# One core, four layers: raw rows sent to the experts and normalised there, the second layer reordered, one barrier, one step and two table waits fewer

## The chip, the cores and the metric

The kernel runs on one core of a Trainium2 chip. A core has five engines that work side by side, each through its own instructions in the order in which they were written: TensorE (matrix products and transposes, into PSUM), VectorE, ScalarE (activations), GpSimd (here small arithmetic and the scatter transfers) and SyncE (it starts transfers). They wait for each other on semaphores. The metric is the device time of one execution in microseconds, the median of several runs. Before the change it is 975.71 us, from 974.56 to 979.03 in three runs.

## The reference

Input `x` is 16 rows of 256 positions of 128 numbers, 4096 tokens. Four layers follow, each a residual around a layer norm (mean and variance over the 128 numbers, no gain):

```python
x = x + attn_a(_layernorm(x))   # q, k, v = x@W + b; 16 heads of 8; softmax within blocks of 64 positions
x = x + ffn(_layernorm(x))      # logits = x@Wr (8 experts); the top 2, softmax of the two;
                                # out = sum of weight * (silu(x@Wg) * (x@Wu)) @ Wd / sqrt(12), hidden 512
x = x + attn_b(_layernorm(x))   # xt = x@w_tor.T + b; q, k, v from xt; attention over the 16 rows of the
                                # input, with a bias of 1 on the diagonal and its two neighbours (cyclic);
                                # then @ out_w.T + out_b
x = x + ffn(_layernorm(x))      # the same expert weights again
```

Everything is fp32. Only the two chosen experts of a token are computed by the kernel.

## The kernel before, in words

Six stages follow each other: `setup`, `first_layer` (first attention, and the routing of its result), `experts`, `second_layer`, `experts` again, and `combine`. `finish` stands between them: GpSimd clears the stage's semaphores, and a barrier over all engines follows (L1790) on top of the one with which a stage's block ends.

**Setup** loads weights and the input (into `stream`, 32 tiles of 128 tokens), folds the torus matrix into Q, K and V, and writes eight empty tiles into the table `routed`.

**First layer.** It works in 16 pairs of tiles; four tiles are a quad, `c = p // 2`. For each `p` every engine has its list, with the work of other quads between: TensorE scores pair p+1, mixes and flips pair p-1 and turns pair p; VectorE takes the maximum (`peak`) and subtracts it (`shift`) for two half groups, divides pair p-2, and in between measures and routes older quads; ScalarE does the exponentials and nearly all copies out of PSUM. Routing of a quad: the sum is measured (`measure2`), GpSimd takes the root (`root2`), VectorE writes a normalised row into `norm_x` (`normalise2`, L672), TensorE transposes it (`turn_x2`) and makes the logits, VectorE finds the top two (`route`), TensorE counts ranks (`route_ranks`), VectorE finds each token's place (`spots`), and GpSimd sends each row twice into `routed` with an indirect DMA (`dispatch`, L441). A row has 132 numbers: the 128, the token, the first expert, and two weights. Beside this the expert weights are loaded and split into a high part (ScalarE, `weight_high`) and a low part (GpSimd, `weight_low`, L434), two a quad from pair 2 to pair 17. At its end a table of which expert and which rows each expert step takes is made.

**Experts.** 72 steps of 128 rows; the steps of an expert follow each other. In a step SyncE loads 128 rows (four buffers; a buffer is free when the step four back is weighed), TensorE transposes them (`turn`), ScalarE and VectorE split them into high and low, TensorE makes gate and up with three products each, ScalarE the Silu (L1669), VectorE the product; TensorE transposes it (`cross`) and multiplies it down; VectorE weighs it and GpSimd scatters the result (L1581). TensorE works one to three steps apart from the others. After four written-out steps it is a loop of four steps a pass.

**Second layer.** It works in eight quads; one round of the lists belongs to a quad `c`, and it is called a step here. The sum of residual and expert results is made (`join`) and goes into `stream`; GpSimd adds the output bias to it (`bias_out`, L1018). TensorE's list in a step: scores(c+1) first half, ranks(c-5), mixing(c-1) first half, two turns, K(c+2), flip(c-1), `turn_back`(c-2), logits(c-4), scores(c+1) second half, mixing second half, Q(c+2), two turns, `map_out`(c-2), V(c+1), flip, `turn_x2`(c-3), `turn_x`(c+3). VectorE's: maximum and shift of the first half (L1302, L1309), divide(c-2) second half, measure, weights and spots of c-5, maximum and shift of the second half, divide(c-1) first half (L1319, L1323), measure2(c-3), route(c-4), join, `add_map`(c-2) (L1331). ScalarE's: Exp first half (L1477), copy of the mixed values, two copies of the turned ones (L1485), K's copies, `out_back`, Exp second half, copy, Q's copy, two copies, the normalisation of c+3 (L1427), V's copies (L1458), the copies of the transposes `out_x2T`(c-3) and `out_xT`(c+3). GpSimd's: `root1`, `bias_out`, two tiles' dispatch of quad c-6, `root2` and a normalisation of quad c-3 (L1011), and two more tiles' dispatch (L1025).

**Combine** loads the two expert results of each token, adds both to `stream` in place, and stores.

## Time and profile before

The profiled execution took 975.18 us, its span (first to last instruction) is 973.4 us, and TensorE's granted clock was 0.88 of full speed in the mean. By the starts of the stages' first transfers:

| stage | from, us | length | TensorE | VectorE | ScalarE | GpSimd | clock |
|---|---|---|---|---|---|---|---|
| setup | 0 | 18.25 | 3.5 | 4.7 | 0.0 | 0.2 | 1.00 |
| first layer | 18.25 | 229.85 | 147.2 | 154.7 | 142.2 | 131.1 | 0.88 |
| experts | 248.10 | 221.80 | 207.0 | 119.4 | 107.3 | 69.0 | 0.97 |
| second layer | 469.90 | 256.50 | 143.8 | 114.4 | 116.8 | 127.0 | 0.75 |
| experts | 726.40 | 221.65 | 206.9 | 119.6 | 107.2 | 69.0 | 0.97 |
| combine | 948.05 | 25.35 | 0.0 | 10.7 | 0.0 | 0.0 | 0.50 |

The engines' columns are busy microseconds. An engine that is busy for nearly the whole stage bounds it; where none is, the order of the waits decides, and the timeline has to be read. A mean over a stage can hide two parts with different bounds, as the second layer does.

### The profile page before, as it was taken

How to read it: one execution, taken by the hardware profiler on the slowest of the kernel's cores; microseconds unless marked ns; L12 is line 12 of the kernel's file. 1: busy time of each engine (PE TensorE's matmuls, PEld its weight loads, DVE VectorE, ACT ScalarE, POOL GpSimd, SP SyncE). 2: the span in 40 equal slices, each digit the busy share in tenths (PEclk: the TensorE clock that was granted, in tenths of full speed). 3: DMA queues.
4: the chain of work that ended last, by engine and by line, in shares of the span. 5: the costliest groups of instructions: out<-in, count | busy, mean ns of one | idle time of the engine just before them, and what ended most of it. 6: DMA issues, size and time to landing. Idle time of an engine off the chain costs nothing. (4 is left out here: it accounts for less than half of the span.)

```text
span 973.4 us, 26881 instructions
## 1 busy us (share of the span) xinstructions
PE 708.4 (73%) x8764; PEld 583.4 (60%) x8765; DVE 523.4 (54%) x1810; ACT 473.5 (49%) x876; POOL 396.2 (41%) x458
## 2 busy tenths in 40 slices
PE   1688877831699999998077898761109999999940
PEld 1356555521588888887035676661108888888830
DVE  3367888863356555554253565642305555555524
ACT  0689877630355555553058897520005555555510
POOL 1223777786033333333231154588732333333320
PEclk9989999975799999999558999985559999999985
DMA  7001222212111111111330000001211111111107
GB/s 204 8 12 45 68 83 87 76 56 67 32 47 47 49 46 47 47 47 36 99 118 24 26 3 10 31 29 39 69 39 41 49 44 49 47 47 49 45 20 259
DMA packets 54045, 54.51 MB, mean 56 GB/s; under 512 B 8272, under 2 KB 43472, under 8 KB 53968
## 3 DMA queue, kind: packets, MB, share of 16 engines
q1 hardware_dynamic: 42608, 32.19, 12.1%
q0 software_dynamic: 8704, 18.11, 5.8%
q10 hardware_dynamic: 2656, 3.15, 0.9%
q8 instruction: 53, 0.87, 0.4%
q14 instruction: 24, 0.20, 0.1%
HBM read 29.51 MB, written 23.90 MB: 55 GB/s over the span
## 5 line engine op out<-in xcount | busy, mean ns | idle before, releaser
L1581 POOL DMA_INDIRECT expert_out<-moe_a_out,moe_a_place x72 | 69.0, 958 | 153.0 <-DVE moe_a_out L1716 153.0
L1581 POOL DMA_INDIRECT expert_out<-moe_b_out,moe_b_place x72 | 69.0, 958 | 152.7 <-DVE moe_b_out L1716 152.7
L1613 PE MATMUL wide<-wgu,moe_a_hi 128*128 x288 | 96.7, 417 | 0.5 <-issue 0.5
L1613 PE MATMUL wide<-wgu,moe_b_hi 128*128 x288 | 96.7, 417 | 0.4 <-issue 0.4
L1629 PE MATMUL wide<-wd,moe_a_hidT 128*128 x576 | 76.4, 276 | 1.1 <-DVE moe_a_out L1716 0.7
L1629 PE MATMUL wide<-wd,moe_b_hidT 128*128 x576 | 76.4, 276 | 1.0 <-DVE moe_b_out L1716 0.7
L1669 ACT ACTIVATE moe_a_glow<-wide 128x512 f32<-128x512 f32 x72 | 43.0, 598 | 69.9 <-PE wide L1613 69.8
L1669 ACT ACTIVATE moe_b_glow<-wide 128x512 f32<-128x512 f32 x72 | 43.0, 598 | 69.6 <-PE wide L1613 69.5
L441 POOL DMA_INDIRECT routed<-la_norm_x,la_place x64 | 63.6, 994 | 23.0 <-issue 19.3
L1629 PEld LDWEIGHTS wide<-wd,moe_a_hidT 128*128 128x128 f32 x576 | 70.0, 192 | 1.7 <-issue 1.7
L1629 PEld LDWEIGHTS wide<-wd,moe_b_hidT 128*128 128x128 f32 x576 | 70.0, 192 | 1.6 <-issue 1.6
L1025 POOL DMA_INDIRECT routed<-lb_norm_x,lb_place x64 | 62.2, 972 | 18.8 <-issue 18.8
L1728 DVE TENSOR_TENSOR moe_a_hid<-wide,moe_a_glow 128x512 f32<-128x512 f32 x72 | 49.8, 691 | 20.4 <-PE wide L1613 17.7
L1728 DVE TENSOR_TENSOR moe_b_hid<-wide,moe_b_glow 128x512 f32<-128x512 f32 x72 | 49.8, 691 | 20.2 <-PE wide L1613 19.1
L1613 PE MATMUL wide<-wgu,moe_a_lo 128*128 x144 | 57.4, 399 | 0.0
L1613 PE MATMUL wide<-wgu,moe_b_lo 128*128 x144 | 57.4, 399 | 0.0
L1613 PEld LDWEIGHTS wide<-wgu,moe_a_hi 128*128 128x128 f32 x288 | 49.5, 192 | 7.5 <-issue 1.0
L1613 PEld LDWEIGHTS wide<-wgu,moe_b_hi 128*128 128x128 f32 x288 | 49.4, 192 | 7.3 <-issue 0.9
L1676 ACT ACTIVATE moe_b_hidT<-wide 128x512 f32<-128x512 f32 x72 | 43.0, 597 | 13.3 <-PE wide L1621 13.3
L1676 ACT ACTIVATE moe_a_hidT<-wide 128x512 f32<-128x512 f32 x72 | 43.0, 597 | 13.1 <-PE wide L1621 13.1
L678 DVE TENSOR_REDUCE la_most<-wide 128x16 f32<-128x1024 f32 x32 | 38.7, 1209 | 19.3 <-PE wide L548 19.2
L1597 PE MATMUL wide<-const,moe_b_rows 128*128 128x128 f32 x72 | 20.0, 277 | 39.7 <-DMA moe_b_rows<-routed 39.7
(257 smaller groups left out, 1693.4 us busy)
## 6 DMA issues: line engine op xcount, KB each, us to landing
moe_a_rows<-routed SPq DMA_DIRECT2D x72, 66.0 KB, 1.9
moe_b_rows<-routed SPq DMA_DIRECT2D x72, 66.0 KB, 1.9
lb_outs<-expert_out SPq DMA_DIRECT2D x8, 512.0 KB
la_stage<-in_wg SPq DMA_DIRECT2D x8, 256.0 KB, 2.6
la_stage<-in_wu SPq DMA_DIRECT2D x8, 256.0 KB, 2.8
wd<-in_wd SPq DMA_DIRECT2D x8, 256.0 KB, 3.7
kept<-stream SPq DMA_DIRECT2D x8, 256.0 KB, 3.6
stream<-kept SPq DMA_DIRECT2D x8, 256.0 KB
```

What stands on the lines that cost most here:

```text
L441: pool.indirect_dma_start(d.routed[:, :], bass.IndirectOffsetOnAxis(ap=place[:, t, j:j + 1], axis=0), norm_x[:, t, :], None).then_inc(sent ...
L678: nc.vector.tensor_reduce(most[gp][:, :], psS[gp][:, :].rearrange("p (h k) -> p h k", k=BLK), X, ALU.max)\
L1025: pool.indirect_dma_start(d.routed[:, :], bass.IndirectOffsetOnAxis(ap=place[:, t, j:j + 1], axis=0), norm_x[:, t, :], None).then_inc(sent ...
L1581: pool.indirect_dma_start(d.expert[:, :], bass.IndirectOffsetOnAxis(ap=place[s % 4][:, 0:1], axis=0), out[u][:, :], None).then_inc(stored[ ...
L1597: nc.tensor.transpose(psX[u][:, 0:P], rows[s % 4][:, 0:D], k.ident).then_inc(turned.sem, 1)
L1613: last = nc.tensor.matmul(ps[u][:, :], x[u][:, :], w(j, part), start=i == 0, stop=i == 2)
L1629: last = nc.tensor.matmul(psY[:, 0:D], hidT[u][:, c * P:(c + 1) * P], k.wd[:, bass.ds(e, 1), c, :].rearrange("p a c -> p (a c)"), start=c ...
L1669: nc.scalar.activation(glow[s % 2][:, :], psG[s % 2][:, :], ACT.Silu).then_inc(glowing.sem, 1)
L1676: nc.scalar.activation(hidT[u][:, :], psH[:, :], ACT.Copy).then_inc(crossed_copied.sem, 1)
L1728: nc.vector.tensor_tensor(hid[u][:, :], psU[u][:, :], glow[u][:, :], ALU.mult).then_inc(hidden.sem, 1)
```

## The change

What it does, part by part:

- *Raw rows.* `norm_x` goes. `stream` gets rows of 134 numbers; the raw sum is what is transposed, sent and kept, and the four numbers of routing and two new ones, the root and minus mean times root, stand behind it. `root2` on GpSimd makes both (four operations for two). The logits of the raw row are multiplied by the root on their way out of PSUM (`take`), and `setup` takes the column means off the router's weights, so that the mean drops out. The expert stages normalise a row tile in place on ScalarE, before the transpose.
- *Second layer.* Ranks, dispatch and so on come one step earlier, dispatching two; every list has a new order. The output bias is added by TensorE: a product of ones with a tile that holds the bias in three bf16 pieces, ahead of the map's products in the same bank. `mix` has two buffers. `join` reads the residual from a tile of its own.
- *First layer.* The spot product and the rest of `spots` are two pieces, the rest behind the second shift; the weights' parts move to the first eight pairs.
- *Seams.* `finish` has no barrier of its own; the next stage takes other semaphores. 71 steps, which is the most that 8192 rows and 8 experts can need. One activation at each stage's head loads ScalarE's table.

The core of the diff:

```diff
-STEPS = 72
+STEPS = 71
-ROW = D + 4
+ROW = D + 6
 def finish(k):
     k.nc.clear_and_free_semaphores(k.used)
+    k.clearing = {s.num for s in k.used}
     k.used = []
-    k.nc.all_engine_barrier()
@@ both layers
+                nc.gpsimd.tensor_scalar(root_in2[u][:, 0, :], mom2[u][:, :, 1], EPS, None, ALU.add)
+                nc.gpsimd.tensor_scalar(root_in2[u][:, 1, :], mom2[u][:, :, 0], -1.0, None, ALU.mult).then_inc(part_rooted2, 1)
+                nc.gpsimd.tensor_tensor(rows[:, :, D + 4], root_in2[u][:, 0, :], ..., ALU.pow).then_inc(part_rooted2, 1)
+                nc.gpsimd.tensor_tensor(rows[:, :, D + 5], root_in2[u][:, 1, :], rows[:, :, D + 4], ALU.mult).then_inc(rooted2, 1)
             def turn_x2(c):
-                pe.wait_ge(normed2, c + 1)
+                pe.wait_ge(summed, 2 * c + 2)          # second layer: c + 1
+            def take(c):
+                dve.wait_ge(logits, c + 1)
+                dve.wait_ge(rooted2, c + 1)
+                nc.vector.tensor_tensor(logit[:, :, :], psX[...], scale.to_broadcast([P, BATCH, EXPERTS]), ALU.mult)
@@ first layer, VectorE, pair p
                 if even and 0 <= c - 3 < QUADS:
-                    weigh(c - 3)
-                    spots(c - 3)
-                if even and 0 <= c - 2 < QUADS:
-                    normalise2(c - 2)
+                    spot_ranks(c - 3)
                 if here:
                     peak(p, 1)
                     shift(p, 1)
+                if even and 0 <= c - 3 < QUADS:
+                    weigh(c - 3)
+                    find_places(c - 3)
@@ first layer, GpSimd (ScalarE's weight_high alike)
-                if 0 <= p - 2 < 2 * EXPERTS:
-                    weight_low(p - 2)
+                if 0 <= p + 1 < EXPERTS:
+                    weight_low(2 * p + 2)
+                    weight_low(2 * p + 3)
@@ second layer, GpSimd
+            for c in range(-3, QUADS + 5):
+                root2(c - 3)
+                dispatch((c - 5) * BATCH + 2), dispatch((c - 5) * BATCH + 3)
+                root1(c + 3)
+                dispatch((c - 4) * BATCH), dispatch((c - 4) * BATCH + 1)
@@ second layer, TensorE (new list)
+  route_ranks(c-4); route_logits(c-3); mixing(c-1,0); score(c+1,0); turn(c,0,0); turn(c,0,1)
+  project_k(c+2); flip(c-1,0); turn_back(c-2); mixing(c-1,1); score(c+1,1); map_out(c-2)
+  turn(c,1,0)  # waits for summed, c - 1, where it waited for back_copied
+  turn(c,1,1); project_q(c+2); flip(c-1,1); project_v(c+1); turn_x(c+3); turn_x2(c-2)
@@ second layer, VectorE (new list)
+  peak(c,0); shift(c,0); spot_ranks(c-4); take(c-3); weigh(c-4); find_places(c-4); measure1(c+3)
+  divide(c-1,0); peak(c,1); shift(c,1); add_map(c-2); route(c-3); count(c-3); measure2(c-2)
+  join(c+4); divide(c-1,1)
@@ second layer, ScalarE: rise_gap(c-4) first, out_xT(c+3) and then out_x2T(c-2) last, the rest as it was
             def map_out(c):
+                nc.tensor.matmul(psP[0]..., k.ones[:, :], k.offset[:, :]...to_broadcast([P, BATCH, D]), start=True, stop=False)
@@ experts, ScalarE
+            nc.scalar.activation(k.warm[:, 4:8], k.warm[:, 0:4], ACT.Silu)
+            def normalise(n, s):
+                row = rows[s % 4]
+                act.wait_ge(loaded[s % 4], (n - s % 4) * 4 + 16)
+                nc.scalar.activation(row[:, 0:D], row[:, 0:D], ACT.Identity, bias=row[:, D + 5:D + 6], scale=row[:, D + 4:D + 5])
+            normalise(0, 0), normalise(1, 1), halve(0, 0), halve(1, 1), normalise(2, 2)
             def step(n, s):
                 ... Silu(s), halve(s + 2), copy of the crossed tile (s - 1) ...
+                if s + 3 < STEPS:
+                    normalise(n + 3, s + 3)
```

(The new lists are written in short here; in the kernel each call has its bounds.)

## Rows read from the trace of the kernel before

**Rows 1.** Busy time by stretch: engine, busy us (instructions); then clock, DMA, GB/s.
```profile
300.00:350.00 50.00, 50.00 (x336) 44.51 (x335) 29.64 (x106) 25.90 (x53) 17.07 (x18) 1.00 0.18 47
570.50:586.40 15.90, 14.78 (x482) 12.29 (x471) 11.04 (x44) 14.21 (x25) 7.65 (x12) 1.00 0.02 4
643.30:717.80 74.50, 15.07 (x148) 13.72 (x140) 21.32 (x139) 3.47 (x9) 59.69 (x66) 0.55 0.16 51
```

**Rows 2.** Timeline (start, us, engine, line), GpSimd, end of the second layer.
```profile
649.74 3.12 POOL L1011 TENSOR_SCALAR lb_norm_x<-stream,lb_mom,lb_rstd 128x128 f32<-128x128 f32 x4
...
716.82 0.96 POOL L1025 DMA_INDIRECT routed<-lb_norm_x,lb_place  x1 [0.30 <-issue]
```

**Rows 3.** The page, parts 5 (costliest groups) and 6 (DMA issues).
```profile
L1669 ACT ACTIVATE moe_a_glow<-wide 128x512 f32<-128x512 f32 x72 | 43.0, 598 | 69.9 <-PE wide L1613 69.8
...
moe_a_rows<-routed SPq DMA_DIRECT2D x72, 66.0 KB, 1.9
```

**Rows 4.** Timeline, GpSimd, one step of the second expert stage.
```profile
928.91 0.96 POOL L1581 DMA_INDIRECT expert_out<-moe_b_out,moe_b_place  x1 [1.87 <-DVE moe_b_out L1716]
```

**Rows 5.** Waits (who for whom: us in total, times, longest), SyncE.
```profile
SPq L1790 <- PEq L1790: 3.0, 6, 0.8
```

**Rows 6.** Timeline, ScalarE, table loads in the two attention layers.
```profile
24.88 1.28 ACT L793 ACT_TABLE_LOAD   x1 [24.88 <-POOL la_nmr L409]
...
512.18 1.28 ACT L1477 ACT_TABLE_LOAD   x1
513.48 1.06 ACT L1477 ACTIVATE lb_prob<-lb_prob 128x1024 f32<-128x1024 f32 x1
```

**Rows 7.** Waits, TensorE, first layer, 83 to 190 us.
```profile
PE wide L484 <- DVE la_spot L737: 4.4, 4, 1.4
```

**Rows 8.** Timeline, GpSimd, end of the first layer.
```profile
217.37 1.25 POOL L434 TENSOR_TENSOR wgu<-la_stage,wgu 128x512 fp32r<-128x512 f32 x1
```

**Rows 9.** Timeline, three engines, attention steps of the second layer.
```profile
529.67 1.05 ACT L1477 ACTIVATE lb_prob<-lb_prob 128x1024 f32<-128x1024 f32 x1
...
568.04 1.07 ACT L1485 ACTIVATE lb_probT<-wide 128x512 f32<-128x512 f32 x2
569.00 1.64 ACT L1427 ACTIVATE lb_norm<-stream,lb_nmr,lb_rstd 128x128 f32<-128x128 f32 x4
570.55 1.22 DVE L1302 TENSOR_REDUCE lb_most<-wide 128x32 f32<-128x1024 f32 x1
571.17 2.55 ACT L1458 ACTIVATE lb_stand<-wide 32x512 f32<-32x512 f32 x4 [0.53 <-PE wide L1081]
574.85 1.31 PE L1183 MATMUL wide<-lb_probT,lb_stand 128*36 128x32 f32 x64
576.09 1.09 PE L1167 MATMUL wide<-const,lb_prob 128*128 128x128 f32 x8
577.02 1.02 PE L1068 MATMUL wide<-lb_xT,wqk_b 128*128 128x512 f32 x2
577.88 0.60 PE L1192 MATMUL wide<-const,lb_side 128*128 128x128 f32 x4
578.52 0.36 DVE L1319 RECIPROCAL lb_inv<-wide 128x32 f32<-128x32 f32 x1 [1.22 <-PE wide L1192]
578.76 0.96 PE L1099 MATMUL wide<-wr,lb_x2T 128*128 128x8 f32 x8
579.03 0.42 DVE L1323 TENSOR_TENSOR lb_mix<-wide,lb_inv 128x256 f32<-128x256 f32 x1
579.87 1.13 PE L1137 MATMUL wide<-lb_kz,lb_qT 32*32 32x128 f32 x64
584.65 1.13 PE L1208 MATMUL wide<-wout,lb_mixT 128*128 128x128 f32 x8 [0.48 <-ACT lb_probT L1485]
585.82 0.69 DVE L1331 TENSOR_TENSOR stream<-wide,stream 128x512 f32<-128x512 f32 x1 [3.18 <-PE wide L1208]
...
626.20 1.05 ACT L1477 ACTIVATE lb_prob<-lb_prob 128x1024 f32<-128x1024 f32 x1
```

More of the change, by code:

```diff
@@ L141, in allocate @@
     k.used = []
+    k.clearing = set()
     def sem(name):
-        k.used.append(nc.alloc_semaphore(name))
+        num = next(n for n in nc.free_semaphores if n not in k.clearing)
+        k.used.append(nc.alloc_semaphore(name, num=num))
         return k.used[-1]
@@ L192, in setup @@
         first = [(raw[:, :, :], d.w_split.rearrange("w c f -> c w f")), (cols[:, :], d.cols), (k.const[:, :], d.const[:, :]),
-                 (k.wout[:, :], d.wout)]
-        first += [(k.rows[:, r, :], d.rows[r:r + 1, :].to_broadcast([P, D])) for r in range(2)]
-        fixed = [(k.stream[:, :, :], d.x.rearrange("(t p) c -> p t c", p=P)), (k.wv[0][:, :], d.wv), (k.wr[:, :], d.wr)]
-        psF, psB = k.bank[0], k.bank[1]
+                 (k.wout[:, :], d.wout), (wr[:, :], d.wr)]
+        first += [(rows, d.rows[r:r + 1, :].to_broadcast([P, D])) for r, rows in enumerate((k.rows[:, :], row[:, :]))]
+        fixed = [(k.stream[:, :, 0:D], d.x.rearrange("(t p) c -> p t c", p=P)), (k.wv[0][:, :], d.wv)]
+        psF, psB, psE = k.bank[0], k.bank[1], k.bank[2]
         @block.sync
@@ L224, in _ @@
             nc.vector.memset(k.ones[:, :], 1.0)
-            for rows in (k.tails, spare):
-                nc.vector.memset(rows[:, :, 0:D], 0.0)
-                nc.vector.memset(rows[:, :, D + 1], -1.0)
-                last = nc.vector.memset(rows[:, :, D + 2:ROW], 0.0)
+            nc.vector.memset(k.warm[:, :], 0.0)
+            nc.vector.memset(even[:, :], 1.0 / D).then_inc(evened, 1)
+            for empty in (k.tails, spare):
+                nc.vector.memset(empty[:, :, 0:D], 0.0)
+                nc.vector.memset(empty[:, :, D + 1], -1.0)
+                last = nc.vector.memset(empty[:, :, D + 2:ROW], 0.0)
             last.then_inc(staged, 1)
+            nc.vector.memset(k.offset[:, :], 0.0)
             dve.wait_ge(weighed, 16 * len(first))
@@ L777, in _ @@
                 if not even and 0 <= c - 2 < QUADS:
+                    take(c - 2)
                     route(c - 2)
@@ L786, in _ @@
         def _(act):
+            nc.scalar.activation(k.warm[:, 4:8], k.warm[:, 0:4], ACT.Exp)
             def normalise1(c):
@@ L1420, in _ @@
         def _(act):
+            nc.scalar.activation(k.warm[:, 4:8], k.warm[:, 0:4], ACT.Exp)
             def normalise1(c):
@@ L1498, in _ @@
             act.wait_ge(cleared, 2)
-            for c in range(-3, QUADS + 6):
+            for c in range(-3, QUADS + 5):
                 here, behind = 0 <= c < QUADS, 0 <= c - 1 < QUADS
+                if 0 <= c - 4 < QUADS:
+                    rise_gap(c - 4)
                 if here:
@@ L1594, in turn @@
                 u = s % 2
-                pe.wait_ge(loaded[s % 4], (n - s % 4) * 4 + 16)
+                normed.wait(pe, n)
                 low.before(pe, n, 2)
@@ L1652, in _ @@
         def _(act):
-            for x in (high, glowing, crossed_copied):
+            nc.scalar.activation(k.warm[:, 4:8], k.warm[:, 0:4], ACT.Silu)
+            for x in (high, glowing, crossed_copied, normed):
                 x.start(act)
+            def normalise(n, s):
+                row = rows[s % 4]
+                act.wait_ge(loaded[s % 4], (n - s % 4) * 4 + 16)
+                nc.scalar.activation(row[:, 0:D], row[:, 0:D], ACT.Identity, bias=row[:, D + 5:D + 6], scale=row[:, D + 4:D + 5])\
+                    .then_inc(normed.sem, 1)
             def halve(n, s):
@@ L1753, in give @@
             eng.wait_ge(joined, n + 1)
-            eng.dma_start(crossed(d.out, n, BATCH), k.stream[:, n * BATCH:(n + 1) * BATCH, :].rearrange("p t c -> p (t c)"))\
+            eng.dma_start(crossed(d.out, n, BATCH), sums[:, n, :, :].rearrange("p t c -> p (t c)"))\
                 .then_inc(stored, 16)
```

351 lines of the change are left out of this document (182 added, 169 removed).

## The prediction

> **What bounds the kernel now.** I read the busy time by stretch first, because the stages have different limits. The expert stages are bound by TensorE: busy for 50.00 us in 50.00, with ScalarE at 25.90 [rows 1]. In the second layer a quad of attention takes 15.90 us, with TensorE at 14.78 and ScalarE at 14.21 busy, so the order on either can decide; after the last quad come 74.5 us in which GpSimd is busy for 59.69 and every other engine is nearly idle [rows 1]. The timeline of that stretch shows GpSimd's work: per quad a normalisation of 3.12 us and eight scatter transfers at 0.96 + 0.30 = 1.26 us each, the last issued at 716.82 and done at 717.8 [rows 2]. So the second layer ends by GpSimd's queue, not by attention. The chain of waits ends in the combine stage, bound by its DMAs, which the change leaves alone. My sums are made on the profiled execution: its span is 973.4 us and its time 975.18, 0.5 us under the median of 975.71.
>
> **Expert stages, both.** *One step fewer:* GpSimd's transfer row gives the period of a step, 0.96 busy + 1.87 idle = 2.83 us [rows 4]. TensorE is full, so each stage loses 2.83: -5.7. *Normalising in the stage:* one 128x128 activation a step; four of them took 1.64, so 0.41 each [rows 9]. ScalarE waits 69.9/72 = 0.97 us a step before the Silu, and the new instruction stands just ahead of that wait. It needs its rows two steps earlier than the transpose does: a row load lands 1.9 us after its issue [rows 3], and it is issued when the weighing four steps back is done, some 3 us before ScalarE comes to it. I cost it at nothing, with that wait and TensorE as its cover. Uncovered it would be 0.41 x 142 = 58 us. At a stage's start nothing covers it, the first transpose waits for the load and then for it: +0.45, twice +0.9 (0 to +1.5, if another load is waited for too). Rows longer by 8 bytes: nothing. Sum -4.8.
>
> **Barriers.** SyncE waited 3.0 us in all for the six barriers that go [rows 5], and the drains before them add a little: -3.2, between -1.5 and -4. GpSimd still clears semaphores, now beside the others; what is late next is its memset, in the second layer under 8 us of loading. The setup's added small VectorE operations lie beside its transfers: nothing, -0.5 to +1.
>
> **Tables ahead.** The first layer's load of 1.28 us stands behind the wait for the first statistics [rows 6]: it goes, -1.3. The second layer's, at 512.18, stands before the first Exp [rows 6]; the walk below deals with it. The Silu load lies beside the first gate matmuls: nothing. 512.18 + 1.28 = 513.46, and the Exp starts at 513.48 [rows 6], so a load costs its 1.28 and no more. The Trainium skill (ScalarE: Activation LUTs, "What ACT_TABLE_LOAD costs") adds a drain of about 1.38 us to every switch to another set, 2.66 in all; by it the two loads would be worth 5.3 us and not 2.6. The trace shows no such drain here, so I go by the trace.
>
> **First layer.** TensorE waited four times, 4.4 us together, for the spot product to free the bank before it could project K [rows 7]. The new order puts that product ahead of the gates' weights, and the normalisation leaves VectorE, so K comes 1.1 us earlier in pairs 8, 10, 12 and 14, which is what ScalarE waits for there: -4.5. Against it, the weights' high parts move to the first eight pairs, where ScalarE is the fuller engine; two copies are 1.07 [rows 9], and pairs 1, 3 and 5 had none: +3.2, less some waiting that takes them up, +2.5. Net -2, between -9 and +4. At the end GpSimd issues 24 transfers with hardly a gap; two low parts of 1.25 that lay among them [rows 8] leave, and the longer second root costs some 0.6: -1.9. With the table -5.2 (-12 to +2).
>
> **Second layer, GpSimd.** The normalisation (3.12 a quad) and the bias go; the root grows from two operations to four, from 1.3 to an estimated 2.0. Per quad 8 x 1.26 + 2.0 = 12.1, where it was 10.1 + 3.1 + 1.4 = 14.6. More important, dispatching starts in step 4 and not in step 6. When attention is done only 36 transfers (half of quad 3, and quads 4 to 7) and three roots are left: 45.4 + 6.1 = 51.5 us. Had attention kept its pace, the second moments of quad 5 would be there 11 us after the Exp at 626.2 [rows 9], at about 637, and the last transfer would be done at 688.5 instead of 717.8: -29.
>
> **Second layer, attention.** I think that it doesn't keep its pace. The new order puts on one chain what ran side by side: the division waits for the flip and now stands before the second maximum; the next scores wait for that shift; the output map stands behind those scores; the second pair of turns waits for the map's sum; Q is projected behind the turns; and ScalarE holds two copies, the next normalisation and V's copies behind Q's. One full step, from the copy of the second transpose to the next one, in the durations of [rows 9]: logits 0.96, mixing 1.31, scores 1.13 + 0.2 for the mask, two turns 1.09, K 1.02, flip 0.60, division 0.36 + 0.42, maximum 1.22, shift the same, scores 1.33, map 1.13 + 0.2 for the bias product, sum 0.69, turns 1.09, Q 1.02 and its copy 0.6, two copies 1.07, normalisation 1.64, V's copies 2.55, the two transposes' copies 0.55 each. That is 22 us, for steps 3 and 4. The bias product (512 columns in bf16) has no row; K is 1.02 for 512 columns in fp32, so it lies between 0.05 and 0.5, and I take 0.2, as for the mask. The other steps leave out what they lack: step 1 has no map, no second transpose and no logits, and its mixing and scores lie before its start (16.8); step 2 adds the map (19.4); step 5 loses the normalisation and its copy (20.0); step 6 has neither K nor Q (17.2). In step 0, Q behind the turns eats what the table gives, so step 1 starts at 529.7 as before [rows 9]. Then 529.7 + 16.8 + 19.4 + 22 + 22 + 20 + 17.2 = 647.1 for step 7, where the old order is at 626.2: 21 us late. The moments of quad 5 follow 11.3 us on, at 658.4, and 51.5 later the last transfer is done: 709.9, which is -7.9. I allow 1 us for stalls that the walk doesn't see: -7, between -29 (pace kept) and +10 (every full step 3 us worse). As a check, the old order walked in this manner gives 15.75 for the step that took 15.90.
>
> **Sum.** -4.8 - 3.2 - 5.2 - 7 = -20.2; 975.2 - 20.2 = 955.0 us.
>
> **The rivals.**
> *Attention keeps its pace.* Steps stay at 16 to 18 us, because the waits that I put in series are met early. For it: TensorE and ScalarE hold about 15 us of work a step [rows 1], so 16 is possible. Against: the orders are fixed in the code, and each link of the chain is a wait there. The layer then gives 29 and not 7: 933.
> *TensorE's clock (the slower side).* A step of 22 us holds 15.5 us of TensorE, 70% of it and not 93%. Where TensorE had 15.07 us in 74.5, it was granted 0.55 of full speed [rows 1], so mostly the lower level of 1.2 GHz. At that level the 11 us of TensorE on the chain would take up to 22: +10 a step. It decides from two such steps (20.2/10); five give 1005. Against: 70% lies nearer to the step that had its full clock than to that stretch.
> *The normalisation is not hidden in the experts.* If the rows came so late that it held up the Silu in every step, +58 us: 1013. Against: 0.97 of wait for 0.41 of work.
> *No change.* The second layer costs 8 us more than I walked and the first loses 4 where it gives 5: about 973.
>
> **Chances.** My forecast 0.70 (its own range 945 to 965); pace kept 0.15; clock 0.06; not hidden 0.03; no change 0.06. The range reaches down to the pace-kept case and up by the bounds of the walk: 934 to 968. 0.5%, 4.9 us, is about what a measurement can tell here. Faster is the first two and half of the last, 0.88; same 0.03; slower 0.09.
>
> **What would show it.** Right: expert steps still of 2.83 us, with ScalarE's wait before the Silu down to about 0.5; no table load ahead of the second layer's first Exp; in its steps 3 and 4 Exps about 22 us apart, with ScalarE idle for some 4 us before the copy of Q; scatter transfers from step 4 on, without a gap once attention is over. Wrong: steps of 16 to 18 us, or a granted clock near one half in them; a Silu that waits for the normalisation; expert steps of more than 2.9 us.

## The result

Median of 20 runs each: 971.47 us (966.28 to 976.82) after, 976.5 us before; the ratio is 0.9953, 95% interval [0.9933, 0.9972]. So the change makes the kernel 0.5% faster, where 955 us, 2.1% faster, was forecast. The profiled execution took 975.08 us over a span of 973.0, 3.6 us above the median of its kernel; the one of before (975.18 us, span 973.4) lies 1.3 us under its own. So the two profiles differ by 0.4 us where the medians differ by 5.0.

The spans cut at ScalarE's first Exp and at GpSimd's first and last transfer of each stage, in us:

| stretch | before | after | difference | forecast |
|---|---|---|---|---|
| start to the first layer's first Exp | 43.3 | 41.8 | -1.5 | |
| last transfer of the first layer to first one of the experts | 23.0 | 24.1 | +1.2 | |
| last one of the experts to the second layer's first Exp (before: with its table load) | 52.9 | 51.0 | -1.9 | |
| last transfer of the second layer to first one of the experts | 22.6 | 23.3 | +0.7 | |
| last transfer of the experts to the end | 34.9 | 33.4 | -1.4 | |
| these seams together | | | -2.9 | -4.9 |
| both expert stages, first to last transfer | 398.2 | 392.0 | -6.1 | -5.7 |
| first layer, first Exp to last transfer | 195.2 | 188.2 | -7.1 | -3.9 |
| second layer, first Exp to last transfer | 203.3 | 219.1 | +15.8 | -5.7 |

(Differences are taken before rounding.) The forecast column holds the prediction's terms, cut at the same places (tables, barriers and the experts' longer starts in the seams); it sums to -20.2, the measured one to -0.3. The expert stages and the first layer came out as well as forecast or better, the seams gained 2 us less, and the second layer took all of it back. A second profile of the same kernel (e4 below, an execution of 969.2 us) has 212.8 us for the second layer, +9.5, and every other row within 0.8 us of the first: what differs between these two executions lies mostly in that layer.

The page after; busy us (share of the span), then forty slices, where PEclk is the granted clock in tenths:

```profile
PE 726.6 (75%) x8736; PEld 594.1 (61%) x8737; DVE 505.1 (52%) x1779; ACT 525.8 (54%) x1016; POOL 363.7 (37%) x446
...
PE   1698898830999999994287677778208999999950
...
PEclk9989999955899999997557978888558999999985
```

What to look at in PEclk is the attention of the second layer, behind the two fives in the middle: 7, 9, 7, 8, 8, 8, 8, where the row of before has 8, 9, 9, 9, 9, 8. TensorE's busy sum rose from 708.4 to 726.6 us with 28 instructions fewer. The second layer more than accounts for the rise, 163.1 us after 143.8 with eight instructions more (the bias products, 0.39 us each): nearly the same matmuls, more of them at the lower clock.

Busy time by stretch, after (engine, busy us, instructions; then clock, DMA share, GB/s), for steps 1 to 6 of the second layer's attention, each from one first-half Exp to the next (the rows that answer to the attention row of [rows 1]):

```profile
519.10:541.10 22.00, 17.75 (x502) 13.16 (x488) 8.73 (x18) 13.12 (x23) 0.64 (x3) 0.77 0.11 27
541.10:559.90 18.80, 11.76 (x334) 9.10 (x315) 9.41 (x19) 13.97 (x25) 3.54 (x6) 1.00 0.01 2
559.90:585.80 25.90, 19.73 (x463) 15.89 (x463) 12.55 (x46) 14.27 (x26) 4.17 (x8) 0.81 0.01 3
585.80:610.10 24.30, 18.36 (x463) 14.86 (x463) 11.98 (x49) 14.22 (x28) 10.38 (x15) 0.86 0.06 20
610.10:633.00 22.90, 17.73 (x459) 14.53 (x459) 10.80 (x41) 12.44 (x23) 8.39 (x11) 0.85 0.08 24
633.00:655.20 22.20, 16.50 (x455) 13.93 (x455) 10.77 (x42) 9.10 (x16) 9.56 (x13) 0.85 0.09 28
```

And two stretches inside them, around the seam of two steps:

```profile
605.80:610.90 5.10, 2.17 (x27) 1.81 (x21) 1.75 (x3) 5.04 (x11) 3.95 (x6) 1.00 0.13 44
610.90:617.70 6.80, 6.80 (x148) 6.04 (x149) 0.91 (x6) 1.52 (x4) 4.26 (x5) 0.50 0.16 45
```

In the first ScalarE is busy for 5.04 of 5.10 us, at what follows the copy of Q in its list (the end of the normalisation, V's copies, two transposes), and TensorE for 2.17, in pieces; in the second TensorE works without a pause at exactly half clock. Five of the six steps hold such a stretch at half clock. The same line at either level, timeline of after:

```profile
586.90 2.05 PE L1208 MATMUL wide<-lb_probT,lb_stand 128*36 128x32 f32 x64
...
594.23 1.31 PE L1208 MATMUL wide<-lb_probT,lb_stand 128*36 128x32 f32 x64 [0.56 <-DVE lb_mix L1349]
```

The first mixing takes 2.05 us, the second, the same 64 matmuls, 1.31. GpSimd's end of the stage is as forecast (timeline, answering [rows 2]):

```profile
669.32 0.24 POOL L1046 TENSOR_SCALAR lb_root_in<-lb_mom 128x4 f32<-128x4 f32 x1 [6.07 <-DVE lb_mom L1323]
669.62 0.23 POOL L1047 TENSOR_SCALAR lb_root_in<-lb_mom 128x4 f32<-128x4 f32 x1
669.93 1.04 POOL L1049 TENSOR_TENSOR stream<-lb_root_in,const 128x4 f32<-128x4 f32 x1
671.05 0.20 POOL L1052 TENSOR_TENSOR stream<-lb_root_in,stream 128x4 f32<-128x4 f32 x1
671.42 1.09 POOL L1058 DMA_INDIRECT routed<-stream,lb_place  x1 [0.16 <-issue]
...
719.95 0.96 POOL L1058 DMA_INDIRECT routed<-stream,lb_place  x1 [0.30 <-issue]
```

From the moments of quad 5 (669.32) to the last transfer's end (720.9) it is 51.6 us; 51.5 was forecast. GpSimd had waited 6.07 us for them: the layer's length was decided by when attention brought quad 5.

The experts, after (costliest groups, answering [rows 3]; timeline, answering [rows 4]; costliest groups again):

```profile
L1719 ACT ACTIVATE moe_a_glow<-wide 128x512 f32<-128x512 f32 x71 | 42.5, 598 | 44.5 <-PE wide L1652 44.5
...
927.49 0.96 POOL L1620 DMA_INDIRECT expert_out<-moe_b_out,moe_b_place  x1 [1.88 <-DVE moe_b_out L1768]
...
L1700 ACT ACTIVATE moe_a_rows<-moe_a_rows 128x128 f32<-128x128 f32 x71 | 34.4, 485 | 1.9 <-DMA moe_a_rows<-routed 1.8
```

A step is still 0.96 + 1.88 = 2.84 us by this row; over the whole stage it is 195.7/70 = 2.80 us, and before it was 199.0/71 = 2.80. The normalisation takes 0.485 us and its rows are there (1.9 us of wait in 71 steps, nearly all of it at the start); the wait before the Silu shrank from 0.97 to 44.5/71 = 0.63.

### The profile page after: what moved, and what is told of

Read it like the earlier page. It is cut to its first block and busy times, and to the rows that moved or that the text cites. A ratio compares the mean times of both kernels' runs of the same rounds, so it can differ in the third digit from the quotient of the medians.

```text
span 973.0 us, 26835 instructions
## 1 busy us (share of the span) xinstructions
PE 726.6 (75%) x8736; PEld 594.1 (61%) x8737; DVE 505.1 (52%) x1779; ACT 525.8 (54%) x1016; POOL 363.7 (37%) x446
## 2 busy tenths in 40 slices
DMA packets 53546, 54.44 MB, mean 56 GB/s; under 512 B 8192, under 2 KB 43008, under 8 KB 53472
## 5 line engine op out<-in xcount | busy, mean ns | idle before, releaser
L479 POOL DMA_INDIRECT routed<-stream,la_place x64 | 62.9, 982 | 29.8 <-issue 16.9
L1058 POOL DMA_INDIRECT routed<-stream,lb_place x64 | 62.2, 972 | 19.9 <-issue 17.9
L1719 ACT ACTIVATE moe_a_glow<-wide 128x512 f32<-128x512 f32 x71 | 42.5, 598 | 44.5 <-PE wide L1652 44.5
L1780 DVE TENSOR_TENSOR moe_a_hid<-wide,moe_a_glow 128x512 f32<-128x512 f32 x71 | 49.1, 691 | 20.6 <-PE wide L1652 18.7
L1726 ACT ACTIVATE moe_b_hidT<-wide 128x512 f32<-128x512 f32 x71 | 42.4, 597 | 12.7 <-PE wide L1660 12.7
L1726 ACT ACTIVATE moe_a_hidT<-wide 128x512 f32<-128x512 f32 x71 | 42.4, 597 | 12.7 <-PE wide L1660 12.7
L710 DVE TENSOR_REDUCE la_most<-wide 128x16 f32<-128x1024 f32 x32 | 38.7, 1210 | 19.0 <-PE wide L587 19.0
L1768 DVE TENSOR_SCALAR moe_a_out<-wide,moe_a_weight 128x128 f32<-128x128 f32 x71 | 24.9, 351 | 37.9 <-PE wide L1668 37.9
```

The costliest lines, as they stand in the source:

```text
L479: pool.indirect_dma_start(d.routed[:, :], bass.IndirectOffsetOnAxis(ap=place[:, t, j:j + 1], axis=0), k.stream[:, t, :], None).then_inc(se ...
L710: nc.vector.tensor_reduce(most[gp][:, :], psS[gp][:, :].rearrange("p (h k) -> p h k", k=BLK), X, ALU.max)\
L1058: pool.indirect_dma_start(d.routed[:, :], bass.IndirectOffsetOnAxis(ap=place[:, t, j:j + 1], axis=0), k.stream[:, t, :], None).then_inc(se ...
L1719: nc.scalar.activation(glow[s % 2][:, :], psG[s % 2][:, :], ACT.Silu).then_inc(glowing.sem, 1)
L1726: nc.scalar.activation(hidT[u][:, :], psH[:, :], ACT.Copy).then_inc(crossed_copied.sem, 1)
L1768: nc.vector.tensor_scalar(out[u][:, :], psY[:, 0:D], weight[s % 4][:, 0:1], None, ALU.mult).then_inc(out_ready.sem, 1)
```

## Experiments: the order of the second layer

**e1, the old order.** TensorE's, VectorE's and ScalarE's lists of the second layer as before, routing five steps behind; everything else of the change stays.

```diff
@@ second layer, TensorE, VectorE and ScalarE: the lists of the kernel before
+  score(c+1,0); route_ranks(c-5); mixing(c-1,0); turn(c,0,*); project_k(c+2); flip(c-1,0); turn_back(c-2)
+  route_logits(c-4); score(c+1,1); mixing(c-1,1); project_q(c+2); turn(c,1,*); map_out(c-2); project_v(c+1)
+  flip(c-1,1); turn_x2(c-3); turn_x(c+3)
@@ second layer, GpSimd
+  root1(c+3); dispatch half of c-6; root2(c-3); dispatch the other half of c-6
```

Expected:

> The kernel after, with the second layer's order of before on TensorE, VectorE and ScalarE and its routing five steps behind; raw rows, bias on TensorE, one barrier a stage, 71 steps and tables ahead stay. Theory (the new order of the attention costs the second layer its gain): the first-half Exps are again 16 to 18 us apart, where they are 19 to 26 apart after, and from the second quad on GpSimd issues 7 quads of 12.1 us without a gap, so the last transfer comes some 15 to 20 us earlier than after (719.95) and the kernel takes about 953 us. Rival (the raw rows or the bias product cost it, not the order): steps stay at 20 us and more, the time at 965 to 975.

Measured: 948.18 us, ratio 0.9711 [0.9661, 0.976]. Steps 1 to 6, from the first-half Exp of quad 1 to that of quad 7, are 98.7 us together (after 136.1; the expectations call this stretch steps 1 to 7, or the seven steps), the last transfer is issued at 692.15, 27.8 us before after's. The theory holds, and gives 5 us more than it said. The raw rows and the bias on TensorE are in this kernel too, so they are not what made after's steps long.

**e2, transfers one step earlier.** `dispatch(c - 5)` for `dispatch(c - 6)` in e1.

> As the kernel with the old order, but GpSimd issues a quad's transfers one step earlier, as soon as its places are there. Theory: the first transfer comes about 7 us earlier, and since GpSimd is the bound from there on, the end does too: about 946 us. Rival (GpSimd then waits for places or for moments in turn, so the queue has gaps): no more than 2 us against the kernel with the old order.

Measured: 937.48 us, ratio 0.9602 [0.9552, 0.9651]. First transfer 6.5 us earlier than in e1, last one 11.0 earlier; the time is 10.7 us under e1's where 7 were expected, so the rival (2 us at most) is out. The profile's steps 1 to 6 are 94.3 us together, 4.4 less than in e1's, and why is open. Its steps (busy time by stretch, steps 2 to 5):

```profile
528.90:543.40 14.50, 12.60 (x407) 10.05 (x408) 7.38 (x13) 13.30 (x24) 0.69 (x2) 1.00 0.02 3
543.40:560.00 16.60, 14.73 (x500) 11.86 (x487) 10.95 (x32) 14.15 (x26) 4.17 (x8) 1.00 0.02 4
560.00:575.70 15.70, 14.48 (x453) 12.05 (x448) 10.04 (x38) 14.16 (x25) 3.40 (x8) 1.00 0.02 5
575.70:594.10 18.40, 15.62 (x478) 12.80 (x479) 10.67 (x41) 12.24 (x22) 9.68 (x12) 1.00 0.11 34
```

In the second and third of these rows ScalarE has the same 14.2 us of work as in a full step of after; TensorE is busy for 14.5 of 15.7 us in the third, and in none of e2's steps 1 to 6 does it lose its clock.

**e3, filled.** In after, the transposes for the logits (four a quad, 32 in the layer) are done four times each into the same place.

```diff
@@ second layer, turn_x2
-                for t in range(BATCH):
+                for t in list(range(BATCH)) * 4:
```

> The kernel after, with each of the 32 transposes for the second layer's logits done four times into the same place: 3 x 0.6 = 1.8 us more TensorE work a step where it waits for ScalarE, nothing else changed. Theory (the gaps make the granted clock fall to one half, and that stretches the chain): no stretch at half clock in steps 3 to 7, each step 2 to 4 us shorter than after (22.2 to 25.9), the kernel 8 to 15 us faster than after, about 960 us. Rival (the order alone makes the step, the clock costs nothing on the chain): steps as long as after or up to 1 us longer, time 971 to 980 us.

Measured: 966.19 us, ratio 0.9902 [0.9867, 0.9938], 5.3 us under after. Half-clock time in steps 1 to 6 fell only from 41.0 to 27.3 us, and the steps sum to 131.7; the second profile of after itself (e4, next) has 30.7 and 130.8, so this profile can't be told from after's. The times can, just: ten runs with a median of 966.2 beside nine of after with 971.9. More work on the same engine made the kernel faster; the direction is the theory's, the size is not.

**e4, after once more.**

> The kernel after once more, for a second profile. If the granted clock in the second layer is what scatters its times (966 to 977 us in runs of the same kernel), this profile shows a different sum of half-clock time in the steps, and steps that differ by 1 us and more from those of the first profile at the same instructions; if the order alone sets them, they are the same within 0.3 us.

Measured: 971.85 us, ratio 0.9961 [0.9922, 1.0001]. The second profile has 30.7 us at half clock in steps 1 to 6, which sum to 130.8 us; its steps 1 and 2 are 18.7 and 18.8 against 22.0 and 18.8, with 3.4 and 0 us at half clock against 10.2 and 0.2. Same instructions, 3.3 us apart in one step, as was expected if the clock scatters the times.

**e5 to e8, and e9, e10, e12.** Beside e5 to e8 the kernel before itself took 1029.2 us instead of 976. In the profiles of these four TensorE stops within groups of matmuls in the attention stages (the last section has the rows); the kernel before was not profiled beside them. Their ratios hold only beside each other, so three of them stand here with their repeats.

**e5 and e10, filled at more places.**

```diff
+            def fill(flats, many):
+                pe.wait_ge(flat_copied, flats)
+                for i in range(many):
+                    nc.tensor.transpose(psP[1][:, i % 4 * P:(i % 4 + 1) * P], k.ident, k.ident)
@@ second layer, TensorE's list of e3, for 0 <= c < QUADS
+  fill(4*c+2, 6) ahead of score(c+1,1); fill(4*c+2, 5) ahead of turn(c,1,0); fill(4*c+4, 6) ahead of turn_x(c+3)
```

> The filled kernel (e3) with idle TensorE time filled at three more places of each step of the second layer: 6 transposes of the identity ahead of the second half's scores, 5 ahead of the second pair of turns, 6 ahead of x's turn, all into a bank that is free there. In after and two variants the sum of steps 1 to 7 goes with the time at half clock: 136.1 us with 41.0 us of it, 130.8 with 30.7, 131.7 with 27.3 (filled). Theory (the chain at full clock is the 117 us that was forecast, and each us at half clock adds about half a us): with under 10 us at half clock the seven steps sum to 118 to 122 us, and the kernel takes 955 to 960. Rival (the chain is longer by its own waits, and the clock only goes along with it): the sum stays at 128 or more however little half-clock time is left, or grows by the fillings.

> The kernel e5 once more, for the same reason. In its run steps 1 and 2 of the second layer had no half-clock time and took 16.7 and 18.8 us (forecast 16.8 and 19.4). Theory (chain as forecast at full clock, plus half a us for each us at half clock): with stops within groups as rare as in the first runs, the seven steps... steps 1 to 6 sum to 117 to 123 us with under 15 us at half clock; the time is 955 to 962 us. Rival: a sum of 128 and more at under 15 us of half clock.

Measured: e5 0.9987 [0.9945, 1.0029], sum 137.8 with 30.7 at half clock and some 20 us of stops; inconclusive. e10: 958.75 us, ratio 0.9847 [0.98, 0.9893], 12.7 us under after, with 29 transposes of 0.15 us more in each full step. The edit only adds work to TensorE, and half-clock time in steps 1 to 6 falls from 41.0 us (30.7 in e4) to 6.8: the gain came through the clock, which so cost after at least 12.7 us by the times, or 10 by the ratios. Its steps 4 to 6 (busy time by stretch):

```profile
575.60:597.70 22.10, 18.85 (x492) 15.74 (x492) 11.96 (x49) 14.34 (x28) 10.72 (x16) 1.00 0.08 24
597.70:618.80 21.10, 18.44 (x488) 15.22 (x488) 10.68 (x41) 12.36 (x22) 8.10 (x11) 1.00 0.08 24
618.80:638.20 19.40, 17.07 (x484) 14.63 (x484) 10.71 (x42) 8.98 (x16) 8.46 (x12) 1.00 0.09 28
```

The steps against the forecast walk, in us, with the part at half clock in brackets:

| step | forecast | after | e4, again | e10, filled |
|---|---|---|---|---|
| 1 | 16.8 | 22.0 (10.2) | 18.7 (3.4) | 18.0 (0) |
| 2 | 19.4 | 18.8 (0.2) | 18.8 (0) | 18.8 (0) |
| 3 | 22 | 25.9 (10.1) | 22.9 (4.4) | 24.6 (6.8) |
| 4 | 22 | 24.3 (6.8) | 25.5 (9.3) | 22.1 (0) |
| 5 | 20 | 22.9 (6.8) | 22.9 (6.8) | 21.1 (0) |
| 6 | 17.2 | 22.3 (6.8) | 22.0 (6.8) | 19.5 (0) |
| sum | 117.4 | 136.1 (41.0) | 130.8 (30.7) | 124.0 (6.8) |

A straight line through seven profiles (after, e4, e11 and e16, which have the same lists in this layer, e12 with its one line moved, e3 and e10 with their fillings) gives 122.6 us + 0.29 us for each us at half clock. So of after's 18.7 us beyond the forecast some 12 (41.0 x 0.29) are the clock and some 6 the chain. The line leans on e10: through the four profiles with the same lists alone it is 123.8 + 0.26, with a correlation of only 0.7. e5's 118 to 122 us was missed by 2 and e10's own 117 to 123 by 1, while its time lay in the expected 955 to 962: the chain is a little longer than forecast, and part of e10's 124 is the fillings, which I can't tell apart from it.

**e7 and e12, one division late.**

```diff
@@ second layer, VectorE
                     shift(c, 0)
+                if 0 <= c - 2 < QUADS:
+                    divide(c - 2, 1)
...
-                if 0 <= c - 1 < QUADS:
-                    divide(c - 1, 1)
```

> The kernel after with one line of VectorE's order put back in the second layer: the second half's division stands behind the next quad's first maximum and shift again. Theory (no single link makes the step; the division in front of that maximum delays the next Exp by what it waits for the flip, up to 1.5 us): steps shorter by 1 to 2 us, the last transfer 5 to 10 us earlier than after. Rival (the map's place between scores and turns is the link that counts): steps within 0.5 us of those of after.

> The kernel e7 once more, for the same reason as e6 again. Theory (that one division is not what makes the step): steps of the second layer at most 2 us shorter than after's, 965 to 970 us. Rival (it is the link that ties each Exp to the flip before it): steps of 17 to 19 us, 955 us or less.

Measured: e7 0.9956 [0.9899, 1.0013], e12 974.66 us, 0.999 [0.9959, 1.002]. No gain, where 965 to 970 us were expected; the steps sum to 136.3 with 48.1 at half clock, as the line gives (136.5). The division in front of the maximum, which my walk put on the chain, gives nothing when it alone is moved.

**e8, the map late too.** `map_out(c - 2)` behind `project_q(c + 2)`, with the old waits.

> The kernel e7 with the output map put back behind Q's projection on TensorE, too. Theory (the chain through map, its sum, the second pair of turns, Q and its copy is the long one): steps fall to 17 to 19 us, and the kernel takes about 953 us. Rival (scores behind mixing, or ScalarE's order, hold the step): steps stay over 20 us.

Measured: 1.0103 [1.0015, 1.019] where e7 beside it had 0.9956. Steps 3 to 6 take 25 to 32 us, and steps 1 to 6 have 62.8 at half clock. The theory is wrong: this made it worse. It was run only where the kernel before took 1029 us, so its size is open.

**e13, Q early.** TensorE projects Q ahead of the second half's scores.

```diff
+                if 0 <= c + 2 < QUADS:
+                    project_q(c + 2)
                 if ahead:
                     score(c + 1, 1)
...
                     turn(c, 1, 1)
-                if 0 <= c + 2 < QUADS:
-                    project_q(c + 2)
```

> The kernel after, with Q's projection in the second layer moved on TensorE from behind the second pair of turns to ahead of the second half's scores, where TensorE waits 1 us for the shift and K's copy is done. ScalarE copies Q ahead of the two turned halves in both. Theory (Q behind the turns is one link of the chain: its 1.0 us and the copies that queue behind it): steps 1 to 7 shorter by 1.0 to 1.5 us each at equal half-clock time, so a sum of about 122 to 127 us instead of 131 to 136, and 960 to 965 us. Rival (the chain runs through map, its sum and the turns, and Q is beside it): within 0.3 us a step and 2 us of after's time.

Measured: 968.28 us (961.4 to 973.42), ratio 0.9926 [0.9896, 0.9956]. The profile sums to 121.4 us with 27.3 at half clock; the line gives 130.5 for that, so 9 us less, 1.5 a step, as expected. But this profile (962.27) is the second fastest of its ten runs. The median gained 3.2 us, which is neither the 960 to 965 of the theory nor the rival's 2 us at most, and its interval overlaps after's.

**e14, scores first.** e13's idea in the old places: scores ahead of the mixing, Q behind the second mixing.

> The kernel after, with TensorE's order of scores, mixing and Q in the second layer as before: each half's scores ahead of the mixing, Q behind the second mixing, all ahead of map and turns. Theory (the scores behind the mixing are the main link: the shift waits for the scores, the Exp for the shift): steps of 17 to 20 us, a sum of 118 to 125 us, 953 to 960 us. Rival (the map ahead of the turns, and VectorE's order, hold the step): no better than the kernel with Q alone moved (e13) by more than 2 us.

Measured: 975.82 us, ratio 1.0011 [0.9984, 1.0038], 4 us slower than after. The rival holds. With map and turns in the new places VectorE waits longer for the map, which now stands behind scores, mixing and Q in TensorE's list (waits, who for whom: us in total, times, longest; 557 to 655 us, e14 and then after):

```profile
DVE stream L1356 <- PE wide L1234: 24.5, 4, 7.8
```

```profile
DVE stream L1356 <- PE wide L1234: 12.7, 4, 4.1
```

So no single link makes the step: the old list is fast as a whole, and pieces of it in the new one gain 3 us or lose 4.

**e6 and e9, the old order with the routing at four steps.** e2 with second transpose and moments two steps behind, logits three, places and transfers four, which is after's depth.

> The early kernel (e2: old order of the attention, transfers as soon as places are there) with only the routing moved one step forward, to the depth that it has in after: second transpose and moments two steps behind the softmax, logits three, places and transfers four. Theory (GpSimd's 8 quads of 12.1 us end the layer from the first transfer on): the first transfer comes about one step, 15 us, earlier than in e2 (580.4), and the last one 10 to 15 us earlier (681.2): about 926 us. Rival (the earlier second transpose puts the map's sum on the chain of the step, as in after, or GpSimd now waits for attention): steps grow from 15.5 to 18 us and more, or gaps of a few us stand between quads; 935 us or more.

> The kernel e6 once more, since in its run every kernel's attention was held up within groups of matmuls that wait for nothing that the profile shows (38.6 us of such stops in the second layer's 180 us here, 7 to 9 us in the first four runs; the kernel before took 1029 us beside it and not 977). Theory: where those stops are rare again, the first transfer comes some 12 to 15 us before e2's (580.4), the last some 8 to 15 us before e2's (681.2), about 927 us. Rival: with the routing at four steps the stops and the longer chain belong to the kernel, not to the run: steps of 18 us and more, 937 us or above.

Measured: e6 0.9849 [0.9773, 0.9926]; e9 937.24 us, 0.963 [0.9582, 0.9677], the same as e2. The first transfer came 13.6 us earlier (566.8), the last one only 1.8 (679.3): steps 3 to 6 grew from 16.5 to 18.9 us on average, and from 542 to 640 us GpSimd waited 36.0 us for places and moments of the second norm (21.3 and 14.7). The rival holds; routing at four steps has nothing to give here.

## Experiments: the other terms

**e11, small parts undone.**

```diff
-STEPS = 71
+STEPS = 72
 def finish(k):
     k.used = []
+    k.nc.all_engine_barrier()
-            nc.scalar.activation(k.warm[:, 4:8], k.warm[:, 0:4], ACT.Exp)      # and the two others
```

> The kernel after with three small parts undone, which show in different places of the trace: 72 steps again in each expert stage, the barrier at each stage's end again, and no activation ahead that loads a table. By the forecast's terms: each expert stage 2.83 us longer from its first to its last transfer (196 to 199 us), 0.4 to 0.9 us more at each of the six stage ends (3.2 us in all), and 1.3 us at the first layer's first Exp; 8 to 11 us in all, so about as slow as before or slower, 980 us. Rival (GpSimd's semaphore clearing now lies on the path, so the barriers took nothing away): under 1 us at the stage ends together, 6 us in all.

Measured: 985.96 us, ratio 1.0102 [1.0052, 1.0151], 14.5 us over after, where 8 to 11 were expected. The expert stages take 198.6 and 199.1 us from first to last transfer (+5.7 together, as forecast). The load ahead of the second layer's first Exp, timeline:

```profile
507.69 1.28 ACT L1512 ACT_TABLE_LOAD   x1
508.98 1.06 ACT L1512 ACTIVATE lb_prob<-lb_prob 128x1024 f32<-128x1024 f32 x1
```

A load costs 1.28 us and nothing around it, here as in [rows 6]. By the Trainium skill (ScalarE: Activation LUTs, "What ACT_TABLE_LOAD costs") it would be 2.66 with its drain, which no run here shows. The seams are 8.8 and 8.9 us longer than in the two profiles of after; less the two tables, 6.3 us are left for the barriers: more than the 3.0 us that SyncE waited in [rows 5]. Against before, e11's seams are longer by 1.3 us at the start, 1.5 and 1.2 at the experts' starts, 1.0 ahead of the second layer and 1.0 at the end. So the barriers gave some 6.3 us and the rest of the change took 6.0 back at the same places. (Between the two profiles of after one seam differs by up to 0.8 us, so the single figures are rough.)

**e15, the bias on GpSimd**, in e2.

> The early kernel (e2) with the second layer's bias added by GpSimd, as before, and no bias product on TensorE. The product takes 0.38 us a quad at full clock, GpSimd's sum 1.4, which lies in the steps before its transfers start. Theory (GpSimd's transfers end the layer, so neither matters much): within 2 us of e2, 937 us. Rival (the product lies on the step's chain): steps shorter by 0.4 us each, 3 us in all, and the first transfer earlier by that; or slower by up to 3 us, if GpSimd's sums delay the statistics of the first layer norm.

Measured: 936.59 us, ratio 0.9607 [0.958, 0.9633]; e2 0.9602. Where the bias is added makes no difference.

**e16, the weights spread** over all pairs of the first layer as before.

> The kernel after, with the experts' weights loaded and split over all pairs of the first layer again, as before, instead of in the first eight pairs. By the forecast the weights early cost 2.5 us in the first eight pairs and save 1 us or so at the end (two low parts among the last transfers), so this kernel's first layer is 1 to 2 us shorter up to its last pair and 1 to 2 us longer behind it: within 1.5 us of after. Rival (splitting late costs ScalarE and GpSimd more than it seems, and the early weights are where the 3 us beyond the forecast come from): the first layer's last transfer 3 to 4 us later than after's.

Measured: 974.92 us, ratio 0.9989 [0.9969, 1.001]. The first layer takes 192.1 us from first Exp to last transfer (after 188.2; the profiles of e1 to e4 and e9 to e15, which have the same first layer, 185.4 to 189.4). From the first to the last Exp it needs 148.2 us, after 149.5; behind the last Exp three low parts of 1.3 us lie among GpSimd's transfers and 43.8 us follow, not 38.7. One of them, timeline:

```profile
204.60 1.28 POOL L470 TENSOR_TENSOR wgu<-la_stage,wgu 128x512 fp32r<-128x512 f32 x1
```

The rival holds: the early weights are worth 4 us, and they are where the first layer gained more than forecast.

## Why the prediction was wrong, step by step

- **Expert stages, -5.7 and hidden normalisation.** Right: -6.1, steps of 2.80 us as before, the wait before the Silu down to 0.63. The normalisation is 0.485 us, not 0.41: the forecast divided the 1.64 us of four in a row by four, but one such instruction in the second layer takes 0.490 us in the mean too, and four in a row overlap. The +0.45 at each start was too small, as far as is known: e11's starts are 1.5 and 1.2 longer than before's, and they were not taken apart.
- **Barriers, -3.2.** Net -0.3 in after with the starts (seams -2.9, less the two tables of 1.3). Two errors that cancel in part: the barriers are worth some 6.3, and setup and starts cost about 6, not 0.9.
- **Tables, -1.3 each.** Right.
- **First layer, -3.9 behind its table.** Measured -7.1. The weights' early place was booked as +2.5, and as part of -1.9 at the tail; e16 shows it as +1.2 up to the last Exp and -5.1 behind it, -4 in all.
- **Second layer, GpSimd.** Right to 0.1 us from the moments of quad 5 on.
- **Second layer, attention.** This is the step that failed. That the new lists make a long chain was right: ScalarE waits 4.4 us a step for Q where "some 4" was forecast (the row below), and the five steps of e10 that kept their clock took 18.0, 18.8, 22.1, 21.1 and 19.5 us where the walk said 16.8, 19.4, 22, 20 and 17.2, 4.1 us more in all, part of it the fillings and 0.2 a step the bias product, which takes 0.39 us and not 0.2. What failed is that the walk took every duration at full clock, on the strength of the sentence against the rival on TensorE's clock, "70% lies nearer to the step that had its full clock". TensorE did lose its clock in five of six steps, for 41.0 us. The busy share of a step, on which that sentence leans, did not tell which: step 2 of after, busy for 11.76 of 18.80 us (63%), kept its full clock, and step 5, busy for 17.73 of 22.90 (77%, its slower matmuls counted at their length), did not. The rival was priced wrongly too: the line makes the clock +2 us a step (12 in six), +3 with the whole excess put down to it, and not +10, for only a part of each step is at the lower level, and VectorE and ScalarE carry part of the chain. Its sign, a granted clock near one half in the steps, did not show either (0.77 to 1.00 in the rows above). Given a chance of 0.06, it was the case that came, at a fifth to a third of its price; my forecast left it out of the walk. The attention came 22.3 us later than the walk to the moments of quad 5: 18.7 in steps 1 to 6, of which some 12 is the clock, 0.8 in step 0 and 2.8 behind the last step, where 6.8 us at half clock lie too. In e4's profile the steps are 13.4 us over the walk and not 18.7.
- **Rows.** Waits of ScalarE after, 559.9 to 655.2 us; before, the same wait was 0.9 us in two:

```profile
ACT lb_qT L1480 <- PE wide L1100: 13.1, 3, 5.4
```

- **Chances.** "Faster" held, by 0.5%. The range ended at 968; the clock case with its true price (+3 in six steps, all of the excess) would have been 973. The case of no change, also 0.06, had 973 as well, by another road (8 us more in the second layer than walked, 9 in the first); the first layer gained more than forecast, so that its figure lies 1.5 us from the median is luck.

Shown by runs: that the order costs the layer its gain (e1, e2), that filling TensorE's pauses gives 10 to 12.7 us back (e10), and that half-clock time and step length differ together between two profiles of the same instructions (after, e4). Only argued: the split of 12 and 6, which rests on a line through seven profiles; a longer chain also leaves more pauses, so along that line cause and effect are not apart. Not settled: which links of the old list it needs; the kernels e8, e12, e13 and e14 show only which ones aren't enough.

The best kernel here is e2 (or e15, or e9, which measure the same): the whole change but for the second layer's lists, 937 us, 4% under before.

## What to carry to other kernels

When a new order makes a longer chain, TensorE can pay twice, by the waits and by its clock: walk the chain at full clock, then ask how much pause per step it leaves on TensorE, look in the profile for how a stretch with such pauses was clocked, and give that case a price in the sum. Shorten a queue that ends a stage (GpSimd's here) without touching the order of the work that feeds it, first. And price a barrier by putting it back into the finished kernel (some 6.3 us here); the wait that the profile shows for it was less than half of that (3.0).

## What the runs showed of the hardware

**The clock fell where no pause was longer than 2.4 us.** In steps 1 to 6 of after 33.2 us of TensorE's pauses of 0.3 us and more lie in 136 us, the longest 2.44, in before 13.5 in 97, in e10 15.6 in 124; the half-clock sums are 41.0, 3.4 and 6.8. The sum of the pauses alone does not set it: e4, the same kernel, has 34.0 us of them and 30.7 at half clock. The Trainium skill (TensorE: Matmul & The Clock Gate, "A second HAM failure mode: psum-queue depth-cycling") tells of a kernel whose short pauses between groups made the clock go up and down; this trace agrees. The same page ("HAM oscillation — how this bites in real kernels") reckons the loss as half of the throttled time; an estimate by it would be 20.5 us for 41.0. The line through the profiles gives 0.29 for each us, 12.

**The scatter between runs goes with the clock.** Over the 20 runs of after, time and mean granted clock go together with a correlation of -0.83: 4.3 us less for each 0.01 of clock. In a span of 973 us 0.01 of mean clock is 19.5 us at half clock, so this makes 0.22 us for each of them, beside the 0.29 of the line. The fastest (966.28 us) had 0.882, the slowest (976.82) 0.865. The four runs each of e1, e2 and e15, with 10.0, 0 and 6.8 us at half clock in steps 1 to 6, lie within 3 us.

**TensorE can stop inside a group.** In e5 to e8 it did so in both attention layers: the first layer takes 211 to 213 us there and 185 to 195 elsewhere, first Exp to last transfer, and the expert stages the same 196. Timeline of e6, one group of scores that waits for no semaphore, and its waits for 524 to 676 us (with "issue", nothing that the profile shows):

```profile
597.80 0.32 PE L1164 MATMUL wide<-lb_kz,lb_qT 32*32 32x128 f32 x2 [0.36 <-issue]
598.55 0.27 PE L1164 MATMUL wide<-lb_kz,lb_qT 32*32 32x128 f32 x1 [0.43 <-issue]
599.28 0.53 PE L1164 MATMUL wide<-lb_kz,lb_qT 32*32 32x128 f32 x2 [0.47 <-issue]
600.69 0.62 PE L1164 MATMUL wide<-lb_kz,lb_qT 32*32 32x128 f32 x2 [0.88 <-issue]
602.11 1.09 PE L1164 MATMUL wide<-lb_kz,lb_qT 32*32 32x128 f32 x5 [0.80 <-issue]
```

```profile
PE wide L1164 <- issue: 11.3, 22, 1.1
```

Gaps of over 0.4 us between one weight load and the next of the same line sum to 39.3 us in e6's second layer (first Exp to last transfer), to 18.0 to 24.5 in e5, e7 and e8, and to 2.4 to 6.5 in all the other profiles, before among them (4.4); none is longer than 1.4 us in e5 to e8. In e6 this group starts while GpSimd issues eight scatter transfers (593.6 to 602.6). The attention's instructions are written out one after the other and the experts' run in a loop, so a slow supply of instructions would explain both; nothing here tests it. A plainer rival is open too: e5 to e8 ran on one chip, the other experiments on three others, where the kernel before took 976 to 977 us.
